# Two products of a filter's factors and six groups of input scalings move from VectorE and ScalarE to GpSimd in the set-up

## The chip, the cores and the metric

The kernel runs on one core of a Trainium2 chip. The metric is the device time of one execution in microseconds (us); less is better. Three runs of the kernel before gave a median of 601.17 us, with 600.91 and 601.51 as the ends.

## The reference, cut to what matters

```
x  = u                                   # (8, 1024, 256) f32
xn = layernorm(x)                        # over the last axis
k  = real(W @ exp(dt * Lam * arange(128)))  # (128 taps, 256 channels): a causal filter
s  = irfft(rfft(k) * rfft(xn)) + xn * D  # convolution along the 1024 positions, per channel
q  = blockwise FP4 quantise + dequantise (16 values share one scale)
h  = silu(q(xn) @ q(w_gate).T) * (q(xn) @ q(w_up).T)   # 704 wide
g  = silu(q(h) @ q(w_down).T)
out = x + s * g
```

The filter is built without its 128 x 256 x 64 exponentials. A tap number is written as a sum of two digits, and the exponential of a sum is a product of two factors. The kernel makes two small tables of factors (`amat`, which also carries the weights W, and `fmat`) as the product of a decaying part (`kk`) and a turning part (`uu`), and one set of matmuls over the 128 rows (64 states, real and imaginary) gives all taps.

## The kernel before, in words

The 8192 rows of the input are 64 tiles of 128 rows by 256 channels. The kernel has a set-up, then a main loop over 32 pairs of tiles, and the last stores. Every engine has its own list of instructions, written out by hand in the order in which it runs, and waits on semaphores that other engines raise; there is no planner. The filter's tables lie in the buffer `xh` that the main loop later fills with the scaled input, and the rounded weights are staged there as well (`gu_hi`, `gu_lo`, `dn_hi`, `dn_lo`), so the order of reuse matters.

What each engine does in the set-up, in its own order:

- SyncE (SP) loads the parameters, the three weight matrices, and the whole input with the rows of every tile reversed into `gbuf` (four loads of 2 MB). Then it loads the first pairs again, unreversed, for the quantised path.
- ScalarE (ACT) makes exponentials and sines of the filter's angles (lines 680 to 698; 28 semaphore increments `k_sin`), squares the weights as the first step of rounding them (702), takes a square root for the norms (704), and then scales groups of four tiles of `gbuf` in place by their 1/std and mean (`a_scale`, line 572, four instructions of 128x256 for one group). In the set-up it scales groups 1, 3, 5, 7, 9 and 11; groups 13 and 15 follow behind step 1 of the main loop, and the eight even groups one in each of steps 0 to 7. It copies the rounded gate and up weights to f16 (`high`, 724) and copies TensorE's transposes to `wgu`.
- GpSimd (POOL) multiplies the weights by their inverse scales (515), then the turning factors by W (521, two instructions of 128x2048) and adds two halves (524, which raises `k_aw`). Then it waits for `k_af`, clears a padding (527), and has nothing more to do until the main loop.
- VectorE (DVE) takes the sines' angles, block maxima of the weights, and the mean and variance of every tile (941, 64 instructions). Then comes a chain of about 30 small instructions on 128x64 numbers and less: mean, variance, 1/std for both orders of rows (lines 946 to 1004; line 1000 raises `nm_ok`, 1004 raises `ln_ok`). Then come the two products that the change moves: `amat` (1009, 2048 numbers, written with a stride of 32 words) and `fmat` (1013, 4096 numbers), which raises `k_af`. Then `round_matrix(0)` and `(1)` (1022, 1024, 1027), `low(0)` and `low(1)` (1034), the first pair's quantisation (`x_first`, `x_second`, `x_parts`: 782 to 862), `round_matrix(2)`, the sum over the filter's matmul (1051 to 1058, after `k_mm`), and the second pair.
- TensorE (PE) waits for `k_af` and `ln_ok`, runs the filter's 64 fp32 matmuls (1175), then transposes the weights (1186) as ScalarE's copies and VectorE's remainders (`w_h`, `w_lo`) come.

In the main loop, one step for a pair: VectorE finds the block scales, multiplies, rounds (796 to 854) and makes high and low parts (888, 862); GpSimd makes the small tables of scales (473 to 491) and, in the first eight steps, the low part of two groups of the input (496, `a_low`) behind ScalarE's high part (582, `a_high`); TensorE does gate and up (1221), transposes (1209, 1230) and the down product (1239, 1241); ScalarE does the activations (605, 609), squares (620) and copies (595, 600). `a_high` of step `it` waits until `a_xs` has reached a count, which says that groups up to `2 it + 1` are scaled.

Semaphores that the change touches: `k_aw` (GpSimd's sum is done), `k_sin` (28 when all exponentials are done), `k_af` (both products are done), `nm_ok` (scale and shift of the reversed rows are there), `a_xs` (a group is scaled).

Of the kernel before, what the change touches and what calls it, by code (L numbers as in the profile page):

```python
# [12 lines left out]
ALU = mybir.AluOpType  # L13
# [6 lines left out]
NT = SEQS * LSEQ // P  # L20
# [13 lines left out]
FH, FA = 4, 8  # L34
# [30 lines left out]
def after(eng, sem, value):  # L65

    if not isinstance(value, int) or value > 0:
        eng.wait_ge(sem, value)

def build(nc, u, u_rev, D, Lre, Lim, logdt, Wre, Wim, wg, wu, wd, out):  # L70
# [5 lines left out]
    with ExitStack() as ctx:  # L76
        ctx.enter_context(nc.allow_non_contiguous_dma(reason="a small load of D"))

        def sb(name, shape, dt):
            return ctx.enter_context(nc.sbuf_tensor(name, shape, dt))  # L80

        def sem(name):
            return ctx.enter_context(nc.semaphore(name))

        xh = sb("xh", [P, NQ, 2, NT, C2], F16)
        gbuf = sb("gbuf", [P, NT, H], F32)
# [37 lines left out]
        def small(words):  # L124
            su[0] += words
            assert su[0] <= 864
            return sm[:, su[0] - words:su[0]]
# [8 lines left out]
        rs_c, nm_c = small(NT), small(NT)  # L136
# [37 lines left out]
        k_sin = sem("k_sin")  # L174
        k_wn = sem("k_wn")
        k_af = sem("k_af")
        k_mm = sem("k_mm")
        k_wt = sem("k_wt")
        k_aw = sem("k_aw")
# [27 lines left out]
        nm_ok = sem("nm_ok")  # L207
        fl_ok = sem("fl_ok")
        ln_ok = sem("ln_ok")
        a_xs = sem("a_xs")  # L210
        a_hi = sem("a_hi")
        a_lp = sem("a_lp")
        x_in = [sem(f"x_in{i}") for i in range(2)]
# [70 lines left out]
        uu = xflat[:, 0:8192].rearrange("p (r h) -> p r h", r=32)  # L284
        kk = xflat[:, 8192:16384].rearrange("p (r h) -> p r h", r=32)
        amat = xflat[:, 8192 + 6144:8192 + 8192]
        fmat = xflat[:, 4096:8192].rearrange("p (b g) -> p b g", g=16)
# [159 lines left out]
        def _(pool):  # L447
            own = Steps(pool, pool_n)
# [74 lines left out]
            own.settle()  # L523
            nc.gpsimd.tensor_tensor(uu[:, 16:24, :], uu[:, 16:24, :], uu[:, 24:32, :], ALU.add).then_inc(k_aw, 1)

            pool.wait_ge(k_af, 1)
            nc.gpsimd.memset(sd_lo[:, :, I:RT * P], 0.0).then_inc(w_pad, 1)

            todo = [(n, part) for n in range(FIRST) for part in range(len(PARTS))]
            made, sent = [0], [0]  # L530
# [36 lines left out]
        def _(act):  # L567
            def a_scale(g):

                for t in range(4):  # L570
                    tile = gbuf[:, bass.ds(g * 4 + t, 1), :].rearrange("p o h -> p (o h)")
                    ins = nc.scalar.activation(tile, tile, ACT.Identity, scale=rs_c[:, bass.ds(g * 4 + t, 1)],
                                               bias=nm_c[:, bass.ds(g * 4 + t, 1)])
                ins.then_inc(a_xs, 1)
# [9 lines left out]
            def x_norm(p, par):  # L584
                act.wait_ge(x_in[par], (p - par) * 8 + 16)
                for t in range(2):
                    tile = xin[1 - par][:, t, :]
                    ins = nc.scalar.activation(tile, tile, ACT.Identity, scale=rstd[:, bass.ds(p * 2 + t, 1)],
                                               bias=nmr[:, bass.ds(p * 2 + t, 1)])
                ins.then_inc(x_n, 1)  # L590

            def x_copy(p, par):
                act.wait_ge(x_tp, p + 1)
                after(act, gu_p, p * 2 - 2)
                nc.scalar.copy(xT[par], p_xT).then_inc(x_tc, 1)

            def h_copy(n, par, src=p_hT):
                act.wait_ge(hT_p, n + 1)
                after(act, dn_p, n - 1)
                nc.scalar.copy(hT[par], src).then_inc(hT_a, 1)  # L600

            def silu_gate(m):
                act.wait_ge(gu_p, m + 1)
                after(act, h_v, m)
                nc.scalar.activation(sg, p_gu[:, 0:I], ACT.Silu, scale=con[:, C_GATE:C_GATE + 1]).then_inc(sg_a, 1)  # L605

            def silu_out(n, t, par, src=None):
                act.wait_ge(dn_p, n + 1)
                nc.scalar.activation(gbuf[:, bass.ds(n, 1), :].rearrange("p o h -> p (o h)"),
                                     p_dn[:, t, :] if src is None else src, ACT.Silu,  # L610
                                     scale=gsc[par][:, t:t + 1]).then_inc(g_a, 1)

            def square(it, pp, x, ch, n):

                if n == 0:
                    after(act, hl_v, it - 1)
                    after(act, x_hl, it * 2 + 4 if x else 2 * NP)
                c = pieces(x, ch)[n]
                act.wait_ge(v_v, pieces_before(it) + (n + 1))
                nc.scalar.activation(d_bf[:, c], by_blk[pp][:, c], ACT.Square,  # L620
                                     scale=float(SQ ** 0.5)).then_inc(sq_a, 1)
# [13 lines left out]
            def step(it, par, x, xt, xn, gu, ch, td, a2=False, cv=False, td1=True, first=True):  # L635

                if td:
                    h_copy(it * 2 - 4, 0)
                    if td1:
                        if a2:  # L640
                            after(act, a_lp, it * 2 - 4)
                        silu_out(it * 2 - 5, 1, 1 - par)
                if a2 and first:
                    a_scale(it * 2)
                if gu and first:
                    silu_gate(it * 2)
                square(it, 1 - par, x, ch, 0)
                if cv and xt:
                    x_copy(it + 1, 1 - par)
                if ch:  # L650
                    square(it, 1 - par, x, ch, 1)
                if xt and not cv:
                    x_copy(it + 1, 1 - par)
                if xn:
                    x_norm(it + 3, 1 - par)
                if td:
                    if a2:
                        act.wait_ge(a_lp, it * 2 - 2)
                    silu_out(it * 2 - 4, 0, par)
                if cv:  # L660
                    y_copy(it * 2 - 2 * S_CONV)
                if td and cv:
                    h_copy(it * 2 - 3, 1)
                if gu:
                    silu_gate(it * 2 + 1)
                if td and not cv:
                    h_copy(it * 2 - 3, 1)
                if a2:
                    if not first:
                        a_scale(it * 2)  # L670
                    scaled = it + 7 if isinstance(it, int) and it < 2 else it + (NT // 8 + 1)
                    a_high(it * 2, scaled)
                    a_high(it * 2 + 1, scaled)
                if ch:
                    down_scale(it - 1, 1 - par)
                if cv:
                    y_copy(it * 2 - 2 * S_CONV + 1)
# [6 lines left out]
            for r in range(8):  # L684
                ins = nc.scalar.activation(uu[:, 24 + r, :], ang, ACT.Identity, scale=float(16 * r), bias=phi[:, 2:3])
# [22 lines left out]
            a_scale(1)  # L708
            act.wait_ge(ln_ok, 1)
            x_norm(0, 0)  # L710
            for n in range(1, 6):
                a_scale(2 * n + 1)

            def weights_out(ns):

# [5 lines left out]
            def high(m):  # L721

                act.wait_ge(w_g, m + 1)
                nc.scalar.copy(gu_hi[m], wraw[:, W_COLS[m]]).then_inc(w_h, 1)

            high(0)
            act.wait_ge(k_pad, 32)
            x_norm(1, 1)
# [14 lines left out]
            x_copy(1, 1)  # L743
            for it in range(PEEL):
                step(it, it % 2, True, it >= 1, True, True, it >= 1, it >= 2, a2=True, td1=it >= 3, first=it >= 1)
                if it == 1:
                    for n in range(6, 8):
                        a_scale(2 * n + 1)
            with act.Fori(0, (S_CONV - PEEL) // 2) as q:
                for par in range(2):  # L750
                    step(q * 2 + (PEEL + par), par, True, True, True, True, True, True, a2=True)
# [19 lines left out]
        def _(dve):  # L771
            own = Steps(dve, dve_n)
            V = nc.vector
# [134 lines left out]
            for n, (r, m, k) in enumerate(rows):  # L908
                ins = V.tensor_scalar(uu[:, r, :], ang, float(m), phi[:, k:k + 1], ALU.mult, ALU.add)
# [21 lines left out]
            for m, (a, b) in enumerate(W_MATS):  # L931
                ins = V.tensor_reduce(mxi[:, m:m + 1], wbm[:, a:b], AX_X, ALU.max)
# [48 lines left out]
            for m, (a, b) in enumerate(W_MATS):  # L981
                ins = V.tensor_scalar(wrs[:, a:b], wbm[:, a:b], minv[:, m:m + 1], XS, ALU.mult, ALU.mult)
# [19 lines left out]
            dve.wait_ge(fl_ok, 1)  # L1002
            own.mark(V.tensor_copy(rstd[:], ps[:, 0:NT]))
            V.tensor_copy(nmr[:], ps[:, NT:2 * NT]).then_inc(ln_ok, 1)

            dve.wait_ge(k_aw, 1)
            a1 = uu[:, 16:24, :]
            dve.wait_ge(k_sin, 28)
            own.mark(V.tensor_tensor(amat.rearrange("p (g h r) -> p r h g", g=16, r=FA),
                                     a1.rearrange("p r (h g) -> p r h g", g=16),  # L1010
                                     kk[:, 16:24, :].rearrange("p r (h g) -> p r h g", g=16), ALU.mult))
            own.settle()
            V.tensor_tensor(fmat, uu[:, 0:16, :].rearrange("p r (h g) -> p (r h) g", g=16),
                            kk[:, 0:16, :].rearrange("p r (h g) -> p (r h) g", g=16), ALU.mult
                            ).then_inc(k_af, 1)

            def round_matrix(m):

# [126 lines left out]
            for n in range(2):  # L1145
                t = NT - 2 + n
# [193 lines left out]
```

## Time and profile before

| | us |
|---|---|
| median of 3 runs | 601.17 |
| the profiled execution, its own time | 602.32 |
| its span, from first to last instruction | 600.5 |
| busy: DVE | 547.2 |
| busy: PE | 478.5 |
| busy: ACT | 404.8 |
| busy: POOL | 199.2 |

The busy time of an engine is the time in which at least one of its instructions runs; the four engines run side by side, so the numbers don't add up to the span. An instruction counts as busy also while it waits for a port. The profiled execution is one run of its own and lies 1.15 us over the median of the runs.

### The profile page before, as it was taken

How to read it: one execution, taken by the hardware profiler on the slowest of the kernel's cores; microseconds unless marked ns; L12 is line 12 of the kernel's file. 1: busy time of each engine (PE TensorE's matmuls, PEld its weight loads, DVE VectorE, ACT ScalarE, POOL GpSimd, SP SyncE). 2: the span in 40 equal slices, each digit the busy share in tenths (PEclk: the TensorE clock that was granted, in tenths of full speed). 3: DMA queues.
4: the chain of work that ended last, by engine and by line, in shares of the span. 5: the costliest groups of instructions: out<-in, count | busy, mean ns of one | idle time of the engine just before them, and what ended most of it. 6: DMA issues, size and time to landing. Idle time of an engine off the chain costs nothing.

```text
span 600.5 us, 13231 instructions
## 1 busy us (share of the span) xinstructions
PE 478.5 (80%) x4956; PEld 334.6 (56%) x4956; DVE 547.2 (91%) x689; ACT 404.8 (67%) x568; POOL 199.2 (33%) x302
## 2 busy tenths in 40 slices
PE   0000357678888899999999999999999888888874
PEld 0000333345556567777777777777777655655653
DVE  6999999889999999899999999999999998998794
ACT  6963856898888876666666666666666654655562
POOL 1093000655555551111111133333332477451400
PEclk9999957879999999999999999999999998989999
DMA  5980012242222345455555555555553399340134
GB/s 175 350 257 1 1 35 88 87 97 89 87 89 88 106 124 158 145 158 149 152 157 158 157 151 150 150 153 157 158 159 89 50 156 156 62 70 1 22 50 70
DMA packets 101186, 70.80 MB, mean 118 GB/s; under 512 B 8848, under 2 KB 100752, under 8 KB 101008
## 3 DMA queue, kind: packets, MB, share of 16 engines
q1 hardware_dynamic: 93072, 61.94, 34.6%
q0 software_dynamic: 8064, 8.13, 9.4%
q8 instruction: 39, 0.64, 0.4%
q14 instruction: 11, 0.09, 0.0%
HBM read 61.28 MB, written 16.91 MB: 130 GB/s over the span
## 4 chain that ended last, share of the span: by engine, by line
PE 49%; DVE 29%; issue 10%; POOL 5%; ACT 3%; DMA 2%; SPq 0%; DVEq 0%; ACTq 0%; POOLq 0%
PE ps L1221 23%; PE ps L1239 8%; PE ps L1241 4%; PE ps L1230 4%; DVE work L854 4%; PE ps L1254 4%; PE ps L1258 3%; DVE wgu L941 3%; DVE work L849 3%; DVE work L888 2%; DVE work L880 2%; DVE sm L796 2%; PE ps L1209 1%; POOL gbuf L506 1%; DVE xh L916 1%
## 5 line engine op out<-in xcount | busy, mean ns | idle before, releaser
L1221 PE MATMUL ps<-wgu,work 128*128 128x512 f16 (+1 forms) x1152 | 247.5, 371 | 7.3 <-DVE work L880 6.1
L1221 PEld LDWEIGHTS ps<-wgu,work 128*128 128x128 f16 x1152 | 113.9, 100 | 119.9 <-issue 17.1
L605 ACT ACTIVATE work<-ps,con 128x704 f32<-128x704 f32 x64 | 54.2, 847 | 116.4 <-PE ps L1221 116.4
L600 ACT COPY work<-ps 128x1408 f16<-128x1408 f16 x64 | 84.9, 1327 | 11.0 <-PE ps L1230 10.7
L1239 PE MATMUL ps<-wdh,work 128*128 128x256 f16 x704 | 89.5, 277 | 2.1 <-ACT work L600 1.4
L849 DVE SCALAR_TENSOR_TENSOR work<-work 128x960 f32<-128x960 bf16 (+2 forms) x67 | 74.0, 1123 | 11.8 <-ACT work L620 11.8
L506 POOL TENSOR_TENSOR gbuf<-gbuf,xh 128x256 f32<-128x256 f32 (+1 forms) x42 | 39.8, 1018 | 107.4 <-DVE work L862 100.1
L1230 PE MATMUL ps<-id,work 128*128 128x128 f16 x704 | 51.0, 222 | 30.1 <-DVE work L888 28.5
L1239 PEld LDWEIGHTS ps<-wdh,work 128*128 128x128 f16 x704 | 66.9, 99 | 10.2 <-ACT work L600 1.6
L854 DVE SCALAR_TENSOR_TENSOR work<-work 128x1920 f16<-128x1920 bf16 (+3 forms) x36 | 69.8, 1939 | 1.2
L815 DVE TENSOR_TENSOR work<-work,ps 128x960 f32<-128x960 f32 (+2 forms) x63 | 68.4, 1126 | 1.1
L880 DVE TENSOR_TENSOR work<-work,ps 128x704 f32<-128x704 f32 x64 | 56.6, 884 | 12.2 <-ACT work L605 10.6
L796 DVE TENSOR_REDUCE sm<-work 128x120 f32<-128x1920 f32 (+2 forms) x32 | 66.4, 2074 | 1.3
L620 ACT ACTIVATE work<-work 128x960 bf16<-128x960 f32 (+2 forms) x67 | 63.0, 963 | 5.8 <-DVE work L815 5.8
L1230 PEld LDWEIGHTS ps<-id,work 128*128 128x128 f16 x704 | 42.1, 99 | 35.7 <-DVE work L888 31.3
L888 DVE TENSOR_TENSOR work<-work,sm 128x1408 f16<-128x1408 f16 (+1 forms) x66 | 54.4, 866 | 7.8 <-DVE work L854 4.4
L496 POOL TENSOR_TENSOR xh<-gbuf,xh 128x1024 f16<-128x1024 f32 x16 | 38.8, 2446 | 47.4 <-ACT xh L582 45.1
L1241 PE MATMUL ps<-wdl,work 128*128 128x256 f16 x384 | 52.4, 273 | 0.0
L473 POOL TENSOR_SCALAR sm<-sm 128x2 int32<-128x2 int32 x31 | 9.9, 321 | 122.1 <-DVE sm L803 122.1
L1254 PE MATMUL ps<-xh,work 128*128 128x64 f16 x768 | 49.1, 192 | 0.3 <-DMA work<-kpad 0.3
L1258 PE MATMUL ps<-xh,work 128*128 128x56 f16 x768 | 49.0, 191 | 0.0
L1254 PEld LDWEIGHTS ps<-xh,work 128*128 128x128 f16 x768 | 42.5, 96 | 3.7 <-DMA work<-kpad 0.4
(153 smaller groups left out, 662.0 us busy)
## 6 DMA issues: line engine op xcount, KB each, us to landing
work<-kpad SPq DMA_DIRECT2D x64, 512.0 KB, 4.0
work<-L_attn_u SPq DMA_DIRECT2D x33, 256.0 KB, 4.8
gbuf<-u_rev SPq DMA_DIRECT2D x4, 2048.0 KB, 17.9
out<-gbuf POOLq DMA_DIRECT2D x7, 1024.0 KB, 9.3
out<-L_attn_u SPq DMA_DIRECT2D x1, 768.0 KB, 5.8
out<-gbuf POOLq DMA_DIRECT2D x1, 768.0 KB, 8.1
work<-L_ffn_w_down SPq DMA_DIRECT2D x1, 704.0 KB, 7.9
work<-L_ffn_w_gate SPq DMA_DIRECT2D x1, 640.0 KB, 4.4
```

The source lines that it names most:

```text
L600: nc.scalar.copy(hT[par], src).then_inc(hT_a, 1)
L796: own.mark(V.tensor_reduce(bm[:, cols], by_blk[pp][:, cols], AX_X, ALU.max, apply_absolute_value=True))
L815: V.tensor_tensor(v, v, sc, ALU.mult).then_inc(v_v, 1)
L849: own.mark(V.scalar_tensor_tensor(v, d_bf[:, c], C0, v, ALU.add, ALU.subtract))
L854: return V.scalar_tensor_tensor(r_f16[:, c], d_bf[:, c], C0, by_blk[pp][:, c], ALU.add, ALU.subtract)
L880: V.tensor_tensor(vb[par][:, I * t:I * t + I], sg, p_gu[:, I:2 * I], ALU.mult).then_inc(h_v, 1)
L1221: last = T.matmul(p_gu[:, a:b], xT[par][:, t, c, :], wgu[:, part, c % 2, a:b], start=(n == 0), stop=(n == len(todo) - 1))
L1230: last = T.transpose(dst[:, c, :], hilo[par][:, t, c * P:c * P + P], id16[:])
L1239: T.matmul(dst, hT[t][:, c, :], wdh[:, c, :], start=(c == 0), stop=False)
L1241: last = T.matmul(dst, hT[t][:, c, :], wdl[:, c, :], start=False, stop=(c == RT - 1))
L1254: T.matmul(dst, tpl[half][:, 2 * c + tp, 0:P], col[:, xp, :], start=(n == 0), stop=False)
L1258: last = T.matmul(dst1, tpl[half][:, 2 * c + tp, P:2 * P], before, start=False, stop=(n == 2))
```

## The change

The two products go from VectorE's list to GpSimd's, directly behind the sum of line 524, and GpSimd now raises `k_af`. GpSimd also scales the groups 5, 7, 9, 11, 13 and 15 (24 `tensor_scalar` instructions of 128x256 f32, behind `nm_ok`), and raises a new semaphore `a_xp` once for each group. ScalarE scales only groups 1 and 3 in the set-up, and no longer 13 and 15 behind step 1; so the copies of the weights (`high(0)`) come right behind group 3. ScalarE now waits for `k_af` ahead of `high(0)`, since the copy overwrites a table that the products read. The count that `a_high` waits for is `it + 3`, and at step 2 ScalarE waits for all six of GpSimd's groups.

```diff
@@ gpsimd, behind the sum that raises k_aw @@
-            pool.wait_ge(k_af, 1)
+            pool.wait_ge(k_aw, 1)
+            pool.wait_ge(k_sin, 28)
+            a1 = uu[:, 16:24, :]
+            own.mark(nc.gpsimd.tensor_tensor(amat.rearrange("p (g h r) -> p r h g", g=16, r=FA),
+                                             a1.rearrange("p r (h g) -> p r h g", g=16),
+                                             kk[:, 16:24, :].rearrange("p r (h g) -> p r h g", g=16), ALU.mult))
+            own.settle()
+            nc.gpsimd.tensor_tensor(fmat, uu[:, 0:16, :].rearrange("p r (h g) -> p (r h) g", g=16),
+                                    kk[:, 0:16, :].rearrange("p r (h g) -> p (r h) g", g=16), ALU.mult
+                                    ).then_inc(k_af, 1)
             nc.gpsimd.memset(sd_lo[:, :, I:RT * P], 0.0).then_inc(w_pad, 1)
+
+            pool.wait_ge(nm_ok, 1)
+            for g in range(5, NT // 4, 2):
+                for t in range(4 * g, 4 * g + 4):
+                    ins = nc.gpsimd.tensor_scalar(gbuf[:, t, :], gbuf[:, t, :], rs_c[:, t:t + 1], nm_c[:, t:t + 1],
+                                                  ALU.mult, ALU.add)
+                ins.then_inc(a_xp, 1)
@@ scalar, step() @@
-                    scaled = it + 7 if isinstance(it, int) and it < 2 else it + (NT // 8 + 1)
+                    scaled = it + 3
+                    if isinstance(it, int) and it == 2:
+                        act.wait_ge(a_xp, NT // 8 - 2)
@@ scalar, set-up @@
-            for n in range(1, 6):
-                a_scale(2 * n + 1)
+            a_scale(3)
@@ scalar, ahead of the weight copies @@
+            act.wait_ge(k_af, 1)
             high(0)
@@ scalar, behind step 1 @@
-                if it == 1:
-                    for n in range(6, 8):
-                        a_scale(2 * n + 1)
@@ vector, behind the small chain @@
-            dve.wait_ge(k_aw, 1)
-            a1 = uu[:, 16:24, :]
-            dve.wait_ge(k_sin, 28)
-            own.mark(V.tensor_tensor(amat..., a1..., kk[:, 16:24, :]..., ALU.mult))
-            own.settle()
-            V.tensor_tensor(fmat, uu[:, 0:16, :]..., kk[:, 0:16, :]..., ALU.mult).then_inc(k_af, 1)
```

## Rows read from the trace of the kernel before

**Rows 1.** The page, part 1: busy time, share of the span, instructions.
```profile
PE 478.5 (80%) x4956; PEld 334.6 (56%) x4956; DVE 547.2 (91%) x689; ACT 404.8 (67%) x568; POOL 199.2 (33%) x302
```
**Rows 2.** Busy time by stretch: from:to, length, each engine, PE's clock, DMA.
```profile
51.00:58.00 7.00, 1.06 (x3) 0.68 (x3) 5.93 (x30) 2.98 (x6) 0.01 (x1) 1.00 0.00 0
58.00:66.00 8.00, 0.08 (x4) 0.09 (x8) 7.97 (x3) 8.00 (x17) 0.08 (x1) 1.00 0.00 1
80.00:90.00 10.00, 6.75 (x39) 3.76 (x37) 8.90 (x14) 4.95 (x8) 0.00 (x0) 0.50 0.16 53
```
**Rows 3.** Chain of waits, 50 to 76 us: start, us, what.
```profile
51.88 0.18 DVE wgu L957
...
57.74 3.68 DVE xh L1009
...
65.78 1.76 DVE work L1022
```
**Rows 4.** Timeline of POOL: start, us, instruction, idle before.
```profile
37.44 8.99 POOL L521 TENSOR_TENSOR xh<-xh,wgu 128x2048 f32<-128x2048 f32 x2
46.51 4.51 POOL L524 TENSOR_TENSOR xh<-xh 128x2048 f32<-128x2048 f32 x1
65.92 0.20 POOL L527 MEMSET xh<- 128x128 f16 x1 [14.91 <-DVE xh L1013]
103.99 0.30 POOL L475 TENSOR_SCALAR sm<-sm 128x32 f32<-128x32 f32 x1 [37.87 <-DVE sm L799]
```
**Rows 5.** Timeline of DVE in the set-up.
```profile
57.65 3.75 DVE L1009 TENSOR_TENSOR xh<-xh 128x2048 f32<-128x2048 f32 x1
61.44 4.43 DVE L1013 TENSOR_TENSOR xh<-xh 128x4096 f32<-128x4096 f32 x1
...
76.29 3.42 DVE L1034 TENSOR_TENSOR xh<-work,xh 128x1536 f16<-128x1536 f32 x2
```
**Rows 6.** Timelines of POOL and DVE around 527 us.
```profile
526.71 0.64 POOL L488 TENSOR_TENSOR sm<-sm 128x240 f16<-128x240 f32 x1
527.32 1.13 POOL L491 TENSOR_SCALAR sm<-sm 128x2 int32<-128x2 int32 x1
...
526.85 1.52 DVE L849 SCALAR_TENSOR_TENSOR work<-work 128x960 f32<-128x960 bf16 x1
```
**Rows 7.** Timeline of steps 0 and 1, DVE and POOL.
```profile
116.32 2.36 DVE L849 SCALAR_TENSOR_TENSOR work<-work 128x960 f32<-128x960 bf16 x2
...
116.47 1.20 POOL L481 TENSOR_TENSOR sm<-sm 128x88 f32<-128x88 f32 x1
...
129.68 0.33 POOL L481 TENSOR_TENSOR sm<-sm 128x88 f32<-128x88 f32 x1
130.08 0.38 POOL L486 CAST sm<-sm 128x240 bf16<-128x240 f32 x1
...
133.26 2.23 DVE L849 SCALAR_TENSOR_TENSOR work<-work 128x960 f32<-128x960 bf16 x2
```
**Rows 8.** One line's instructions: count, duration in ns min/median/max, first and last start.
```profile
L849 DVE SCALAR_TENSOR_TENSOR work<-work x67: 687/1158/1517, 82.8 to 586.3; 128x960 f32<-128x960 bf16 x58, 128x704 f32<-128x704 bf16 x6, 128x512 f32<-128x512 bf16 x3
...
L815 DVE TENSOR_TENSOR work<-work,ps x63: 687/1147/1156, 104.3 to 567.1; 128x960 f32<-128x960 f32 x58, 128x704 f32<-128x704 f32 x4, 128x512 f32<-128x512 f32 x1
...
L941 DVE BATCH_NORM_STATS2 wgu<-gbuf x64: 400/405/416, 30.3 to 50.9; 128x6 f32<-128x256 f32 x64
...
L506 POOL TENSOR_TENSOR gbuf<-gbuf,xh x42: 733/756/1924, 350.8 to 564.7; 128x256 f32<-128x256 f32 x28, 128x512 f32<-128x512 f32 x14
```
**Rows 9.** Timelines of ACT and PE.
```profile
71.15 1.47 ACT L724 CAST xh<-work 128x1536 f16<-128x1536 f32 x1 [1.46 <-DVE work L1027]
...
123.00 4.04 ACT L572 ACTIVATE gbuf<-gbuf,sm 128x256 f32<-128x256 f32 x8
...
116.38 3.74 PE L1221 MATMUL ps<-wgu,work 128*128 128x512 f16 x18 [1.42 <-DVE work L880]
...
124.78 6.68 PE L1221 MATMUL ps<-wgu,work 128*128 128x512 f16 x18 [0.77 <-DVE work L880]
```

More of the change, by code:

```diff
@@ L210, in build @@
         a_xs = sem("a_xs")
+        a_xp = sem("a_xp")
         a_hi = sem("a_hi")
@@ L1004, in _ @@
             V.tensor_copy(nmr[:], ps[:, NT:2 * NT]).then_inc(ln_ok, 1)
-            dve.wait_ge(k_aw, 1)
-            a1 = uu[:, 16:24, :]
-            dve.wait_ge(k_sin, 28)
-            own.mark(V.tensor_tensor(amat.rearrange("p (g h r) -> p r h g", g=16, r=FA),
-                                     a1.rearrange("p r (h g) -> p r h g", g=16),
-                                     kk[:, 16:24, :].rearrange("p r (h g) -> p r h g", g=16), ALU.mult))
-            own.settle()
-            V.tensor_tensor(fmat, uu[:, 0:16, :].rearrange("p r (h g) -> p (r h) g", g=16),
-                            kk[:, 0:16, :].rearrange("p r (h g) -> p (r h) g", g=16), ALU.mult
-                            ).then_inc(k_af, 1)
             def round_matrix(m):
```

## The prediction

> **What bounds the kernel now.** I read the page's busy times first, then the busy time by stretch over the set-up, then the chain of waits there, and last the timelines of the engines that the change touches. Over the whole span VectorE is the busiest engine with 91%, GpSimd the idlest with 33% [rows 1]. In the stretch that the change touches it is clearer still: from 58 to 66 us VectorE is busy for 7.97 of 8.00 us and from 51 to 58 us for 5.93 of 7.00, while GpSimd does nothing [rows 2]. The chain of waits runs there on VectorE alone: the small statistics instructions from 51.7 us, the first product at 57.74, the second, and the first rounding instruction at 65.78 [rows 3]. So a microsecond taken from VectorE between 51 and about 104 us, when step 0 begins, is a microsecond of the kernel, and one added to it is too. The main loop behind it doesn't change, so the set-up's shift is carried to the end.
>
> **What the change takes away.** VectorE loses the two products. The chain counts them from 57.74 to 65.78 us, that is 8.04 us [rows 3]; alone they took 3.75 and 4.43 us [rows 5]. By that alone the time would be 602.3 - 8.0 = 594.3 us in the terms of the profiled execution.
>
> **What GpSimd's products take.** Line 524, a GpSimd product-like instruction of 128x2048 f32 with two inputs, took 4.51 us, and line 521 took 8.99 for two of them [rows 4]. So `amat` is 4.5 and `fmat`, twice as long, 9.0 us. `amat` is written with a stride, which on VectorE made it 3.75 us where half of `fmat` is 2.22 [rows 5]; no GpSimd row shows a strided write. I bound it by 4.5 us and by 4.5 x 3.75 / 2.22 = 7.6, and take 4.5, since GpSimd at 2.2 ns a number is already slower than VectorE was with the stride (1.83 ns). Line 524 ends at 51.02 us [rows 4], so the products run from 51.1 to about 55.7 and on to 64.8 us. By themselves they would be in time: `k_af` would come 1 us earlier than before (65.9).
>
> **What they do to VectorE.** This decides. GpSimd's instructions and those of VectorE that take two inputs from SBUF don't run at the same time. Row by row: the GpSimd product of line 481 takes 0.33 us when it is undisturbed (129.68) and 1.20 us when it comes in 0.15 us behind a rounding instruction of VectorE (116.32): it ends just behind that instruction [rows 7]. The other way round, a rounding instruction that starts at 526.85, inside a GpSimd instruction that runs from 526.71 to 527.35, takes 1.52 us where the median is 1.16; it is held for 0.37 us and so reads only from 527.2 on [rows 6, 8]. That is the whole of what was left of the GpSimd instruction but for its last 0.13 us. VectorE's instructions that read PSUM for one input never show it: line 815 has 1156 ns as its maximum over 63 instructions, with a median of 1147 [rows 8]. Nor do those with one input: the 64 statistics instructions stay within 400 to 416 ns [rows 8], though GpSimd's long products of lines 521 and 524 run beside most of them [rows 4].
>
> The trace holds nothing longer than 0.5 us in which VectorE waits, so the price for a product of 9 us is bounded: below by nothing, above by the whole of it. I take the whole, since both directions in the rows last as long as the other's instruction does. The Trainium skill says the same in "SBUF — State Buffer", section "Who interferes with whom": the shared pair of ports is locked for a full instruction by whichever starts first, and a VectorE instruction with two SBUF inputs contends with a GpSimd instruction that reads SBUF. The trace agrees where it can, with the 0.37 us; that it holds for a 9 us instruction no row here shows. It is the rule that speaks against this change.
>
> Now the order. Of the chain of small instructions, line 956 and the next ones have two SBUF inputs. Line 956 was at 51.70, line 957 at 51.88 [rows 3]; `amat` has been running since 51.1, so line 956 is held until 55.6. GpSimd waits for its own `amat` to complete before `fmat`, some 0.1 us; one to three of the small instructions (0.18 us each) slip through, then `fmat` takes the ports until 64.8. The rest of the small chain was 57.74 - 51.88 = 5.86 us long [rows 3] and now runs from 64.8 to 70.6. Then `round_matrix(0)` starts at 70.6 instead of 65.78: **+4.8 us**. In other words VectorE gets back 8.0 us and is held for 12.9. The bounds of this term are -8.0 (no holding) and +4.8 + 3.1 = +7.9 (slow `amat`).
>
> What is queued behind line 956: `nm_ok` and `ln_ok`, so ScalarE's square root and scalings, GpSimd's own scalings and TensorE's filter matmul start about 13 us, 13 us, 13 us and 5 us later. ScalarE has now 8 scalings less (groups 1 and 3 remain, 8 instructions of about 0.5 us, as 8 took 4.04) [rows 9], and with them and `x_norm` it is done about 75 us, before `round_matrix(0)` ends at 75.9. So `high(0)` isn't late for any other reason than VectorE, and the new wait for `k_af` at 64.8 costs nothing.
>
> **What the 24 scalings on GpSimd do.** They start at about 69.6 us and have idle time until 104 [rows 4], so they hide for GpSimd. No row shows such an instruction. Bounds: 0.38 us like the one-input cast of 240 numbers, and 0.76 like the two-input product of 256 [rows 7, 8]; I take 0.5, nearer to the one-input row, and they last until about 85 to 90 us. "GPSIMD Engine Reference", section 3.1 of the Trainium skill, gives about 1.8 cycles a number at best, which at 1.2 GHz would be an estimate of 0.38 us plus the dispatch. In that stretch VectorE has 18 instructions with two SBUF inputs: six of `round_matrix(0)` and `(1)`, two of `low`, seven of the first pair's quantisation, three of `round_matrix(2)`. Between each two of them one scaling slips in (24, less two before them and some four beside reductions and reciprocals, is 18 as well). What one costs VectorE: the pair of line 849 with one GpSimd instruction between took 2.36 us, without it 2.23 [rows 7], so 0.13 us for a GpSimd instruction of 2 x 88 numbers. A scaling of 256 numbers reads more, so some 0.17 us: 18 x 0.17 = **+3.0 us**. Bounds: nothing, and 18 x 0.76 = 13.7.
>
> **What ScalarE gains.** Ten microseconds of scalings leave its set-up and 4.04 us leave the place behind step 1 [rows 9]. In the set-up it was waiting for VectorE at line 724 (1.46 us idle before it) [rows 9], so this is worth nothing. Behind step 1 its next work, the copy of the transposes, could come 2.9 us earlier, but TensorE runs the gate product from 124.78 to 131.5 [rows 9] before it uses that copy. Worth 0; what hides it is that product. If TensorE's gate product ran at full clock (3.74 instead of 6.68 us) [rows 9] ScalarE would be late in the old order, and 1 us might show.
>
> **TensorE's clock.** From 80 to 90 us the granted clock was 0.50, that is 1.2 of 2.4 GHz [rows 2], after little work; the same 18 matmuls took 3.74 us in step 0 and 6.68 in step 1 [rows 9]. A shifted set-up can move one such product across the border: +-3 us, which I give the range, not the sum.
>
> **The sum.** +4.8 + 3.0 + 0 = +7.8 us. From the profiled 602.3 us that gives 610.1; the median of the runs lies 1.15 us lower, so 609.0 us.
>
> **The rivals.**
>
> First, the faster one: the lock isn't held through a long GpSimd instruction, and VectorE's small reads slip between its parts. For it: no row shows a hold over 0.5 us. Against it: rows 6 and 7. VectorE would reach `round_matrix(0)` at 57.7; `k_af` would come at 64.8, `high(0)` (1.47 us) [rows 9] be done at 66.3, before VectorE has finished both matrices at 68.2, and `low(0)` would start at 68.2 instead of 76.29 [rows 5]. That is the full 8.1 us, less some 1 us for scalings: 594 to 595 us. It decides if VectorE is held for less than 8.0 - 3.0 = 5.0 us in all between 51 and 66 us.
>
> Second, half of it: VectorE is held by `amat` (3.9 us) but gets its small chain through ahead of `fmat` or beside it. Then -8.0 + 3.9 + 3.0 = -1.1, 600 us.
>
> Third, worse than the forecast: the scalings take GpSimd 0.76 us or more and each holds VectorE for about 0.6 us, or `amat` is slow. 18 x 0.6 = 10.8 instead of 3.0: 617 us; with a slow `amat` alone 612.
>
> **How the numbers follow.** Full hold with cheap scalings 0.70 (609.0, by itself 604 to 614); costly scalings or much of it 0.12 (614 to 618); no hold 0.12 (594); half a hold 0.06 (600). I predict 609.0 us. From 603.5 to 616 us lies the first case with the clock's 3 us on both sides and most of the third, about 0.8. A difference of 0.2%, 1.2 us, is what can be told from no change. Slower by more than that 0.81, within it 0.04, faster 0.15.
>
> **What would show it.** In the changed kernel's timeline VectorE's line of the first statistics sum (956 before) should start at 51.7 and last some 4 us, one of its next neighbours some 9 us, and the first rounding instruction start at about 70.6. The mean of the rounding instructions (lines 1022 to 1027 before) should rise from 1.76 to about 1.9. If the small chain still ends at 57.7, the first rival holds; if the rounding instructions last over 2.3 us, the third. If ScalarE's `high(0)` starts long after the first matrix is rounded, I missed a wait.

## The result, and the profile after

The changed kernel takes 607.12 us (median of four runs, 606.94 to 607.73) where the kernel before takes 601.31 (four runs). The ratio is 1.0099, with a 95% interval of 1.0082 to 1.0117: 5.8 us slower. The prediction was 609.0 us, with a range of 603.5 to 616.

The span of the profiled execution grows from 600.5 to 605.1 us, by 4.6; the profiled execution of the kernel before was a slow one, 1.0 us over the median, so the medians are the better measure. Part 1 of the page after, which answers to [rows 1]:

```profile
PE 477.0 (79%) x4956; PEld 334.8 (55%) x4956; DVE 553.8 (92%) x687; ACT 393.6 (65%) x544; POOL 241.4 (40%) x328
```

VectorE has two instructions less and yet is busy for 6.6 us more. Its two products were 8.2 us of busy time, so some 15 us came in from elsewhere, and VectorE was given no new work. Busy time by stretch, after, which answers to [rows 2] (from:to, length, PE, PEld, DVE, ACT, POOL, PE's clock, DMA):

```profile
51.00:58.00 7.00, 0.26 (x1) 0.18 (x1) 6.93 (x7) 0.00 (x0) 6.84 (x3) 1.00 0.00 0
58.00:66.00 8.00, 0.00 (x0) 0.00 (x0) 7.88 (x8) 0.50 (x2) 7.05 (x2) 1.00 0.00 0
```

From 51 to 58 us VectorE ran 30 instructions before, busy for 5.93 of 7.00 us, and 7 now, busy for 6.93. A high share with few instructions is how a held engine looks in such a table. The timeline of POOL after, and under it that of DVE; they answer to [rows 4, 5]:

```profile
46.50 4.51 POOL L525 TENSOR_TENSOR xh<-xh 128x2048 f32<-128x2048 f32 x1
51.09 4.53 POOL L530 TENSOR_TENSOR xh<-xh 128x2048 f32<-128x2048 f32 x1
55.69 9.21 POOL L534 TENSOR_TENSOR xh<-xh 128x4096 f32<-128x4096 f32 x1
64.85 0.20 POOL L537 MEMSET xh<- 128x128 f16 x1
69.32 31.11 POOL L542 TENSOR_SCALAR gbuf<-gbuf,sm 128x256 f32<-128x256 f32 x24 [4.27 <-DVE sm L1016]
```

```profile
51.14 0.26 DVE L962 TENSOR_REDUCE work<-ps 3x1 f32<-3x128 f32 x1
51.43 4.25 DVE L964 COPY work<-work 3x128 f32<-3x128 f32 x1
55.62 0.25 DVE L972 TENSOR_TENSOR wgu<-wgu 128x64 f32<-128x64 f32 x1
...
56.26 8.84 DVE L976 TENSOR_SCALAR wgu<-wgu 128x64 f32<-128x64 f32 x1
64.88 0.22 DVE L977 SCALAR_TENSOR_TENSOR wgu<-wgu 128x64 f32<-128x64 f32 x1
...
70.19 1.83 DVE L1027 SCALAR_TENSOR_TENSOR work<-work 128x1536 f32<-128x1536 bf16 x1
72.05 2.00 DVE L1029 SCALAR_TENSOR_TENSOR work<-work 128x1536 f32<-128x1536 bf16 x1
74.09 2.00 DVE L1032 TENSOR_TENSOR work<-work 128x1536 f32<-128x1536 f32 x1
```

The same copy and the same `tensor_scalar` in the kernel before:

```profile
51.49 0.21 DVE L948 COPY work<-work 3x128 f32<-3x128 f32 x1
...
52.28 0.20 DVE L960 TENSOR_SCALAR wgu<-wgu 128x64 f32<-128x64 f32 x1
```

Read them side by side. A copy of three rows (line 964), 0.21 us before, lasts 4.25 us and ends as the product `amat` ends (55.6). Three small two-input instructions (lines 972 to 974, with no wait between them) slip through at 0.25 us each, though the record of `fmat` starts 0.3 us ahead of the last of them. A `tensor_scalar` of 64 numbers in each row (976), 0.20 us before, lasts 8.84 us and ends 0.2 us behind `fmat` (64.9). Together the two wait for 12.7 us. The first rounding instruction starts at 70.19 us instead of 65.78 [rows 3]. The chain of waits of the changed kernel carries both (start, us, what):

```profile
51.43 4.25 DVE work L964
...
56.26 8.84 DVE wgu L976
...
70.19 1.84 DVE work L1027
```

Marks of VectorE, read from the timelines of both kernels: the first rounding instruction at 65.8 before and 70.2 us after (+4.4); the start of the filter's sum (line 1051, now 1056) at 89.8 and 96.2 (+6.4); the first full-sized reduction, of step 0, at 109.06 and 115.75 (+6.7). The same reduction of step 1 starts at 124.73 and 131.36 (+6.6), that of step 2 at 141.04 and 146.63 (+5.6). Three of the gate and up products, PE after:

```profile
107.52 5.66 PE L1226 MATMUL ps<-wgu,work 128*128 128x512 f16 x18
115.79 3.73 PE L1226 MATMUL ps<-wgu,work 128*128 128x512 f16 x18 [2.61 <-DVE work L896]
...
131.41 5.64 PE L1226 MATMUL ps<-wgu,work 128*128 128x512 f16 x18 [0.20 <-DVE work L896]
```

The second of these took 5.41 us before, 2.9 of them at a granted clock of 0.50 (1.2 of 2.4 GHz), and 3.73 now, at 1.00; that gave nothing, as the shift is 6.6 us at step 1 too. The third took 6.68 us before (124.78) [rows 9], at a mean granted clock of 0.55, and 5.64 now, at 0.65. The chains of waits of both kernels go through it, and it is where the shift falls by 1.0 us.

### The profile page after: what moved, and what is told of

Read it like the earlier page. It is cut to its first block, busy times and chain, and to the rows that moved or that the text cites. A ratio compares the mean times of both kernels' runs of the same rounds, so it can differ in the third digit from the quotient of the medians.

```text
span 605.1 us, 13229 instructions
## 1 busy us (share of the span) xinstructions
PE 477.0 (79%) x4956; PEld 334.8 (55%) x4956; DVE 553.8 (92%) x687; ACT 393.6 (65%) x544; POOL 241.4 (40%) x328
## 4 chain that ended last, share of the span: by engine, by line
PE 50%; DVE 31%; issue 9%; POOL 3%; ACT 3%; DMA 2%; SPq 0%; DVEq 0%; ACTq 0%; POOLq 0%
PE ps L1226 24%; PE ps L1244 8%; PE ps L1246 5%; PE ps L1235 4%; DVE work L870 4%; PE ps L1259 4%; PE ps L1263 4%; DVE wgu L957 3%; DVE work L865 3%; DVE work L896 2%; DVE work L904 2%; DVE sm L812 2%; DVE wgu L976 1%; PE ps L1214 1%; DVE work L831 1%
## 5 line engine op out<-in xcount | busy, mean ns | idle before, releaser
L1235 PEld LDWEIGHTS ps<-id,work 128*128 128x128 f16 x704 | 41.6, 98 | 35.4 <-DVE work L904 31.1
L1246 PE MATMUL ps<-wdl,work 128*128 128x256 f16 x384 | 53.7, 277 | 0.0
```

The source lines that it names most:

```text
L1235: last = T.transpose(dst[:, c, :], hilo[par][:, t, c * P:c * P + P], id16[:])
L1246: last = T.matmul(dst, hT[t][:, c, :], wdl[:, c, :], start=False, stop=(c == RT - 1))
```

## The experiments

All were run beside the kernel before, whose median in those runs was 600.7 to 600.8 us. A time in brackets is the difference to it. "Step 0" is the start of VectorE's first full-sized reduction, 109.06 us before; it is free of what TensorE's clock does later.

**products_only.** The change without the scalings on GpSimd; ScalarE keeps them.

```diff
-            a_scale(3)
+            for n in range(1, 6):
+                a_scale(2 * n + 1)
```

> Only the two products go to GpSimd; the six groups stay on ScalarE. Theory (VectorE is held by GpSimd's products): the first rounding instruction starts at about 70.2 us as in the change, and ScalarE, whose scalings start 13 us later with it, is now late: six groups and one x_norm from 69.2 last until about 82.6, so the first weight copy is late and low(0) waits. Worse than the change: about +8 us over before, 609 to 610. Rival A (the cost is in the scalings on GpSimd, not in the products): about 594 to 601. Rival B (the cost is in ScalarE's new wait for k_af): the same as the change or better, since k_af comes at 65.

607.88 us (+7.1; ratio 1.0113, 1.0094 to 1.0133), step 0 at 116.6 (+7.5). I had expected +8. Rival A, that the cost is in the scalings on GpSimd, falls. The rounding starts where it does in the change, and ScalarE is late with its copies:

```profile
70.17 1.76 DVE L1021 SCALAR_TENSOR_TENSOR work<-work 128x1536 f32<-128x1536 bf16 x1
...
83.54 1.76 DVE L1033 TENSOR_TENSOR xh<-work,xh 128x1536 f16<-128x1536 f32 x1 [2.77 <-ACT xh L733]
85.90 1.76 DVE L1033 TENSOR_TENSOR xh<-work,xh 128x1536 f16<-128x1536 f32 x1 [0.60 <-ACT xh L733]
```

Most of the cost is in the products. The second half of the change repairs a part of what the first half breaks: scale and shift numbers that come 12.5 us later make ScalarE's scalings late. At step 0 the repair is worth 0.8 us; the medians can't tell the two kernels apart, as their intervals overlap.

**products_unscaled, scalings_only and neither_unscaled.** A table of two by two: the products on GpSimd or VectorE, and the six groups on GpSimd or scaled by nobody. The last of the four is the change itself.

```diff
 products_unscaled: as products_only, but
+            a_scale(3)                      # and groups 5 to 15 (odd) nowhere
 scalings_only: the change, with the two products back on VectorE
 neither_unscaled: the kernel before, but
-            for n in range(1, 6):
-                a_scale(2 * n + 1)
+            a_scale(3)
```

> The two products on GpSimd, groups 5 to 15 (odd) scaled by nobody (left out of the computation). Theory: the hold alone, first rounding instruction at 70.2 us, nothing added behind it: +4.4 at the end of the set-up and some 4 us in all, 604.5 to 606; the difference to the change, some 2 us, is what 24 scalings on GpSimd take from VectorE. Rival A (the scalings cost it all): 594 to 601.

> Only the six groups go to GpSimd; the products stay on VectorE. Theory: 24 scalings from 56.7 us on slip between VectorE's two-input instructions, 0.1 to 0.2 us each; the products themselves are only two instructions, so some 2 to 2.5 us over before: 603 to 604. Rival C (ScalarE's relief is worth something): 600 or less. Rival A: +5 to +6 us, 607.

> The kernel before with groups 5 to 15 (odd) scaled by nobody (left out of the computation): what ScalarE's relief is worth alone. Theory: nothing, within 0.5 us of before, 601.3. Rival C (ScalarE was on the path in the set-up or behind step 1): 597 to 600.

| | step 0, us | time, us | ratio and interval |
|---|---|---|---|
| neither_unscaled | 109.05 (0.0) | 600.46 (-0.4) | 1.0003, 0.9991 to 1.0016 |
| products_unscaled | 113.50 (+4.4) | 604.44 (+3.6) | 1.0061, 1.0039 to 1.0083 |
| scalings_only | 111.25 (+2.2) | 602.43 (+1.6) | 1.0026, 1.0013 to 1.0040 |
| the change | 115.75 (+6.7) | 607.12 (+5.8) | 1.0099, 1.0082 to 1.0117 |

The change's time is set against its own kernel before (601.31). At step 0 the two parts add up to the whole: 4.4 + 2.2 = 6.6. ScalarE's relief is worth nothing that can be measured. The 24 scalings cost 2.2 us with or without the products. In time, scalings_only came out lower than expected (603 to 604). Their durations, in the change (ns, min/median/max):

```profile
L542 POOL TENSOR_SCALAR gbuf<-gbuf,sm x24: 544/551/5219, 69.3 to 99.9; 128x256 f32<-128x256 f32 x24
```

Undisturbed they take 0.55 us; 24 of them take 31.1 us instead of 13.2, so more than half of that is waiting for VectorE. The longest was passed over by three of VectorE's instructions, the last rounding one of the second matrix and the pair of line 1039:

```profile
80.12 5.22 POOL L542 TENSOR_SCALAR gbuf<-gbuf,sm 128x256 f32<-128x256 f32 x1
```

What VectorE pays for one is the step from 1.76 to 2.00 us in its rounding instructions; over the six of the first two matrices the mean is 1.92.

**late_products.** As products_unscaled, but GpSimd waits until VectorE's small chain is done, so that its products fall on the large rounding instructions.

```diff
             pool.wait_ge(k_aw, 1)
+            pool.wait_ge(ln_ok, 1)
```

> As products_unscaled (604.4 us, +3.6), but GpSimd starts the products only when VectorE's small chain is done (ln_ok, about 57.6 us). Theory (the ports are held for each whole instruction, wherever it falls): the first rounding instruction starts at 57.7, amat then holds the second from 59.4 to 63.9, fmat the third from 65.7 to 74.9: two waits of 4.5 and 9.2 us instead of 4.3 and 8.8, the second matrix is rounded at 82 instead of 76.4 before, +5.6 us there, 604.5 to 606.5 in all. Rival D (it is the chain of small instructions that is sensitive; big ones stream beside GpSimd): rounding ends at 68.2, ScalarE waits for k_af at 71.4, low(0) at 73: -3 us, 597 to 598.

604.54 us (+3.8; ratio 1.0070, 1.0050 to 1.0090). The timeline of VectorE:

```profile
57.66 1.76 DVE L1018 SCALAR_TENSOR_TENSOR work<-work 128x1536 f32<-128x1536 bf16 x1
59.45 5.97 DVE L1020 SCALAR_TENSOR_TENSOR work<-work 128x1536 f32<-128x1536 bf16 x1
65.46 10.24 DVE L1023 TENSOR_TENSOR work<-work 128x1536 f32<-128x1536 f32 x1
75.62 1.75 DVE L1018 SCALAR_TENSOR_TENSOR work<-work 128x1536 f32<-128x1536 bf16 x1
```

The same price at another place: 1.76 us instructions last 5.97 and 10.24, and GpSimd's `amat` lasts 5.99 instead of 4.53, as VectorE's first instruction was there before it. Whole instructions take turns, also when both are large. The second matrix is rounded at 81.0 us; 82 was expected. Rival D, that large instructions stream beside GpSimd (597 to 598 us), falls.

**memset_products and late_memsets.** GpSimd only writes: four memsets of 128x4096, once at the place of the change's products and once behind the small chain. The products are left out.

```diff
-            own.mark(nc.gpsimd.tensor_tensor(amat...))
-            nc.gpsimd.tensor_tensor(fmat...).then_inc(k_af, 1)
+            for n in range(4):
+                ins = nc.gpsimd.memset(xflat[:, 12288:16384] if n == 0 else xflat[:, 4096:8192], 0.001)
+                ...                             # behind the first three: wait until it is done
+            ins.then_inc(k_af, 1)
```

> As products_unscaled, but GpSimd's two products are replaced by four memsets of 128x4096 f32 (each some 3.6 us, 14.5 in all; the products and the scalings of six groups are left out): GpSimd is as long busy and raises k_af as late (65.7 us), but reads nothing from SBUF. Theory (VectorE's second input meets GpSimd's reads): no two-input instruction of VectorE is held; the first rounding instruction starts near 57.7 us, -8 us: 592.5 to 594. If one-input instructions that were held by the products (the copy, 4.25 us, and the tensor_scalar, 8.84 us) are held by a memset too, since they write by the shared port, up to 8 of the 14.5 us come back: 597 to 604. Rival E (any busy GpSimd holds VectorE): as products_unscaled, 604.4 or 1 us more.

> As late_products (604.5 us), but with memset_products' four memsets of 128x4096 in place of the products (they and the scalings of six groups are left out). GpSimd only writes, from 57.8 to 72 us, beside VectorE's rounding instructions, which have two SBUF inputs and need one write port. Theory (two inputs meet reads; one-input instructions in SBUF meet reads and writes): the six rounding instructions take 1.76 us each, rounding ends at 68.2 us instead of 76.3, ScalarE is then late by its wait for k_af (72.0): low(0) at 73.5, -3 us: 597 to 598. Rival (a GpSimd write holds every SBUF instruction of VectorE): the second rounding instruction is held some 3.6 us, and so are the next ones, 604 or more.

memset_products: 604.28 us (+3.6; ratio 1.0068, 1.0047 to 1.0089). GpSimd's memsets run from 51.09 to 65.31 us, and VectorE's small chain is held in four places:

```profile
51.45 3.22 DVE L952 COPY work<-work 3x128 f32<-3x128 f32 x1
...
54.77 3.44 DVE L964 TENSOR_SCALAR wgu<-wgu 128x64 f32<-128x64 f32 x1
...
58.63 3.13 DVE L973 TENSOR_SCALAR work<-work 128x3 uint32<-128x3 uint32 x1
...
62.23 3.38 DVE L986 TENSOR_SCALAR work<-work 128x96 f32<-128x96 f32 x3
```

My first branch (-8 us) fell, the one that I had put second holds, and higher than I thought: every memset holds one copy or `tensor_scalar`, even one of three numbers in each row. The time alone also fits rival E, that any busy GpSimd holds whatever VectorE does; the other run decides that. late_memsets: 599.20 us (-1.6; ratio 0.9975, 0.9963 to 0.9988), and there the two-input instructions run through four memsets (57.88 to 72.10 us) undisturbed:

```profile
59.53 1.76 DVE L1018 SCALAR_TENSOR_TENSOR work<-work 128x1536 f32<-128x1536 bf16 x1
61.32 1.76 DVE L1021 TENSOR_TENSOR work<-work 128x1536 f32<-128x1536 f32 x1
...
73.64 1.76 DVE L1028 TENSOR_TENSOR xh<-work,xh 128x1536 f16<-128x1536 f32 x1 [5.30 <-ACT xh L731]
```

So there are two kinds. An instruction of VectorE with two SBUF inputs is held by a GpSimd instruction that reads and not by one that only writes. A copy or `tensor_scalar` from SBUF to SBUF is held by either. Rounding ended at 68.3 us, 8 us early; ScalarE's wait for `k_af` then gave 5.3 us back. 597 to 598 us was expected: `low(0)` starts 2.65 us early as forecast, but 1.2 of them are lost behind it, where VectorE waits for ScalarE again (step 0 is at 107.58, -1.5). That wait costs nothing in the change only because VectorE is later still.

**fmat_in_pieces.** As products_unscaled, with `fmat` as 16 instructions.

```diff
-            nc.gpsimd.tensor_tensor(fmat, uu[:, 0:16, :]..., kk[:, 0:16, :]..., ALU.mult).then_inc(k_af, 1)
+            for r in range(16):
+                ins = nc.gpsimd.tensor_tensor(xflat[:, 4096 + 256 * r:4352 + 256 * r], uu[:, r, :], kk[:, r, :], ALU.mult)
+            ins.then_inc(k_af, 1)
```

> As products_unscaled (604.4 us), but fmat is made by 16 instructions of 128x256 instead of one of 128x4096. Theory (held for one instruction, then the other engine gets its turn): no wait of VectorE is over 0.8 us behind amat; the longest, 8.84 us, goes; small instructions and pieces take turns, VectorE's fixed part and its reciprocals run beside GpSimd, so the first rounding instruction starts at 67 to 68.5 us instead of 70.2: 601.5 to 603.5. Rival (GpSimd keeps the ports through back-to-back instructions): 604.4 as before, one wait of about 9 us.

601.51 us (+0.8; ratio 1.0017, 1.0002 to 1.0033), 2.8 us better than with one `fmat`. The wait in line 966 (8.69 us with one `fmat`) is gone, and many short ones have come:

```profile
56.28 0.61 DVE L966 TENSOR_SCALAR wgu<-wgu 128x64 f32<-128x64 f32 x1
...
56.95 0.71 DVE L968 TENSOR_SCALAR wgu<-wgu 128x64 f32<-128x64 f32 x1
57.70 0.68 DVE L970 TENSOR_TENSOR wgu<-wgu 128x64 f32<-128x64 f32 x1
...
66.40 1.76 DVE L1017 SCALAR_TENSOR_TENSOR work<-work 128x1536 f32<-128x1536 bf16 x1
```

GpSimd pays for it: its 16 pieces take 13.0 us instead of 9.2, and VectorE gets on 3.8 us earlier. The hold is for one instruction, and its length is the length of GpSimd's.

**amat_only_early, early_psum and early_sines.** Towards a better kernel. Only `amat` moves, and GpSimd's list is shifted to where VectorE's instructions have one SBUF input and are neither copies nor `tensor_scalar`s: the 64 statistics.

```diff
 amat_only_early
+            dve.wait_ge(k_wn, 1)                    # VectorE: copy of W ahead of the weight maxima
+            V.tensor_copy(wt, ps[:, 0:512]...).then_inc(k_wt, 1)
             dve.wait_ge(s_w, 16 * 5)
 GpSimd: lines 521 and 524, then 515, then
+            nc.gpsimd.tensor_tensor(amat..., a1..., kk[:, 16:24, :]..., ALU.mult).then_inc(k_am, 1)
 early_psum, besides
-        wbm, wrs = scratch(WW // BLK), scratch(WW // BLK)
+        wbm, wrs = ps[:, 1536:1536 + WW // BLK], scratch(WW // BLK)
 early_sines, besides: angles, turns and sines in the order 2, 3, 0, 1 instead of 0, 1, 2, 3
-            pool.wait_ge(k_sin, 4)
+            pool.wait_ge(k_sin, 2)
```

> A version meant to be better than both: only amat goes to GpSimd, and VectorE's copy of the W table stands ahead of its weight maxima, so that GpSimd takes the W products from 26.2 us (sines done), the weights' product behind them, and amat at about 47.8 to 52.4 us, mostly beside the one-input statistics that aren't held. Scalings stay on ScalarE. Theory: VectorE loses 3.75 us of work and is held for some 0.9 us: -2.5 to -3 us, 598 us; the weights' squares on ScalarE come 10 us later (52 us) and still before the rounding. Rival: VectorE's W copy or the later squares delay the square root by more than 1 us, or the reduction of the weights is held by GpSimd: 600 to 603.

> amat_only_early (604.3 us) with one difference: the weights' block maxima (wbm, 128x280 f32) lie in PSUM, so that the two tensor_scalar instructions that were held for 3.3 and 4.3 us beside GpSimd's products read PSUM. Theory (only an instruction with all its operands in SBUF uses the second port): both take about 0.3 us again, the statistics start at 30.3 us as before, only the copy behind them is held for 0.9 us by the last of amat, the first rounding instruction starts at 62.9 to 63.1 us instead of 65.8: -2.9 us, 597.5 to 598.5 (a clock step of 1 to 2 us either way). Rival (GpSimd's products slow all of VectorE's one-input work): as amat_only_early, +3.5.

> early_psum with the angles and sines of the last 16 rows made first, so that GpSimd's W products start at 22.7 instead of 26.4 us and amat ends at 48.9, ahead of the copy behind the statistics. Theory: nothing of VectorE is held, the first rounding instruction starts at 62.0 us, -3.75 against before: 597 to 597.8, 0.9 us better than early_psum. Rival: the reordered angles or the two-input STT of the angles beside GpSimd cost it back: as early_psum.

amat_only_early missed (598 was expected): 604.29 us (+3.6; ratio 1.0061, 1.0040 to 1.0082). I had looked for collisions behind the statistics, and there was a pair ahead of them. Its two `tensor_scalar`s of 280 numbers, 0.30 us each before, beside GpSimd's W products:

```profile
27.50 3.53 DVE L937 TENSOR_SCALAR work<-work 128x280 f32<-128x280 f32 x1
30.96 4.62 DVE L938 TENSOR_SCALAR work<-work 128x280 f32<-128x280 f32 x1
```

The same two in early_psum, where they read PSUM, with the same GpSimd instructions beside them (from 26.34 to 35.35 us):

```profile
27.49 0.45 DVE L937 TENSOR_SCALAR work<-ps 128x280 f32<-128x280 f32 x1
27.86 0.45 DVE L938 TENSOR_SCALAR ps<-ps 128x280 f32<-128x280 f32 x1
```

early_psum: 597.45 us (-3.3; ratio 0.9951, 0.9934 to 0.9968), faster than both kernels, with nothing of the computation left out. Rounding starts at 62.85 us, 2.9 us early as expected. early_sines: 597.30 us (-3.5; ratio 0.9959, 0.9943 to 0.9976), rounding at 62.39. It gains the 0.5 us by which the copy behind the statistics was still held (0.69 instead of 0.21 us), and in the time that can't be told from early_psum. I had expected 0.8 to 0.9.

## Why the prediction was right

**The hold.** The term that decides, +4.8 us, was measured as +4.4 at the first rounding instruction and at step 0 (products_unscaled). The two waits were put at 3.9 and 9.0 us and are 4.0 and 8.6, without the instructions' own 0.2. That the rows showed only 0.4 us of holding, and the products would hold for 13, was an extrapolation; late_products and fmat_in_pieces show it at two other places and lengths. `amat` took 4.53 us with its strided write, so the lower bound was right. (The code puts neighbouring numbers 128 words apart, not 32.)

**Which instruction is held.** Here the working was wrong in detail. I named line 956, which has two inputs, and wrote that instructions with one input never wait, from the 64 statistics. The copy in front (948) and the `tensor_scalar` (960) were the ones held. The statistics are one-input instructions too, but of another kind. The sum came out by the luck that in this chain one instruction stands behind the other, so that it doesn't matter which link is held. Where it does matter, in amat_only_early, the same gap in the reasoning cost me the expectation by 6 us. The Trainium skill has both kinds apart in "SBUF — State Buffer", section "Who interferes with whom": two-port modes of copy, cast and `tensor_scalar` contend with anything of GpSimd, two SBUF inputs only with its reads. The runs agree with the first half in memset_products (3.1 to 3.4 us), and with the second in late_products (5.97 and 10.24 us) and late_memsets (1.76 us throughout). I had read the second half only.

**The scalings.** +3.0 forecast, 2.2 measured. The single instruction was sized well (0.5 forecast, 0.55 measured) and so was VectorE's price for one (0.17 forecast, 0.24 in the rounding instructions). What failed is "between each two of them one scaling slips in": line 1039, two instructions without a wait between, took 3.41 us, the same as before, while the scaling of 80.12 us waited. GpSimd comes in mainly where VectorE waits for its own result. By the measured price, 2.2 us are an estimate of nine such places, where I had counted 18.

**ScalarE.** Worth 0 as forecast, in the set-up and behind step 1 (neither_unscaled, 1.0003). The working had a slip that costs nothing for that reason: the set-up loses not 8 scalings and ten microseconds but 16 scalings, which took 7.9 us. The new wait for `k_af` was free (ScalarE reached the matrix at 76.2 us, `k_af` was there at 64.9).

**The clock.** Left out of the sum and given 3 us of range. Between the reductions of steps 1 and 2 the shift falls from 6.6 to 5.6 us, in the one gate and up product shown above. That this comes from the change isn't shown: in neither_unscaled, whose time is that of the kernel before, the same product starts 0.1 us later than before and takes 5.87 us instead of 6.68.

**The sum.** The measured terms at step 0 are 4.4 + 2.2 = 6.6 us, where +7.8 was forecast. The medians differ by 5.8 us, with an interval of 4.9 to 7.0 from the ratio's. So the forecast was 1.9 us high: 0.4 by the hold, 0.8 by the scalings, and the rest behind step 0, where the cause stays open.

The first rival (no hold, 594 us) and the second (half) fell with products_unscaled. Of the third, costly scalings fell with the 0.55 us and the slow `amat` with the 4.53 us.

## What to carry to other kernels

Work moved to an idle GpSimd isn't free for VectorE: what GpSimd does in SBUF is bought with the time of certain VectorE instructions, whole instruction by whole instruction. A long GpSimd instruction costs the same whether the one that it holds is tiny or large. Before such a move, list what VectorE does in that window: reductions, statistics and `tensor_scalar`s that read PSUM run beside it; copies and `tensor_scalar`s in SBUF don't, nor do two-input instructions in SBUF while GpSimd reads. Move the GpSimd work into the first kind of window, put small operands of the others in PSUM, or cut GpSimd's instruction in pieces (which here only made the loss smaller, +0.8 instead of +3.6 us).

## What the runs showed of the hardware that I had not expected

- A GpSimd memset, which reads nothing, makes a `tensor_scalar` of 128x3 numbers last 3.13 us instead of 0.17, and lets a two-input instruction of 128x1536 pass at 1.76 us.
- An input in PSUM takes a `tensor_scalar` of 128x280 from 3.53 us beside a GpSimd product to 0.45 (line 937), and input and output in PSUM take another from 4.62 to 0.45 (938); alone and in SBUF each is 0.30.
- Two VectorE instructions without a semaphore wait between them aren't parted by a waiting GpSimd instruction in line 1039 of the change (3.41 us for two, as before). The pair of line 878 pays beside the scalings (0.93 instead of 0.76 us), and in the main loop of the kernel before a pair was parted once (2.36 instead of 2.23 us) [rows 7]. What decides stays open.
